# Softmax attention: key differences as units of the score ring, eight visits of 512 queries, head outputs added by GpSimd

## The reference

```
h = layernorm(x, ln1_g, ln1_b)
q, k, v = (h @ Wq), (h @ Wk), (h @ Wv)            # 16 heads of 16
scores = einsum('bqhd,bkhd->bhqk', q, k) / sqrt(16)
attn   = softmax(scores, axis=-1)                  # over 4096 keys
ctx    = einsum('bhqk,bkhd->bqhd', attn, v)
x = x + ctx @ Wo
```

## Time and profile before

| | us |
|---|---|
| median of 3 runs (lowest, highest) | 3835.98 (3832.73, 3839.26) |
| the profiled execution's own time | 3843.38 |
| its span | 3841.6 |
| PE busy | 3525.6 (92%) |
| DVE busy | 2883.9 (75%) |
| ACT busy | 2607.8 (68%) |
| POOL busy | 735.7 (19%) |
| mean granted TensorE clock | 0.944 |

### The profile page before, as it was taken

One profiled execution on the slowest core, in us unless ns is written; L12 is line 12 of the kernel. 1 busy time (PEld: TensorE's weight loads), 2 busy tenths in 40 slices (PEclk: granted clock), 3 DMA queues, 4 the chain that ended last, 5 costly groups with the idle time before them and its releaser, 6 DMA issues. The chain is left out here.

```text
span 3841.6 us, 86736 instructions
## 1 busy us (share of the span) xinstructions
PE 3525.6 (92%) x29108; PEld 1910.1 (50%) x29108; DVE 2883.9 (75%) x5446; ACT 2607.8 (68%) x3034; POOL 735.7 (19%) x735
## 2 busy tenths in 40 slices
PE   7979999999999999999999999999998807999990
PEld 4534444444444444444444444444443706999980
DVE  1767999999999999999999999999994522333335
ACT  2427888888888888888888888888887104555540
POOL 0300000000000000000000000000000367888856
PEclk8958999999999999999999999999999758999995
DMA  3630101010110101011010101101001524444424
GB/s 108 219 66 11 26 12 26 14 24 14 24 26 13 25 14 24 14 24 26 14 24 14 24 14 26 24 14 24 13 13 49 180 102 140 139 139 137 137 86 131
DMA packets 159912, 206.72 MB, mean 54 GB/s; under 512 B 50177, under 2 KB 123777, under 8 KB 154369
## 3 DMA queue, kind: packets, MB, share of 16 engines
q1 hardware_dynamic: 141136, 173.78, 16.7%
q0 software_dynamic: 6336, 16.79, 1.4%
q10 hardware_dynamic: 12144, 12.06, 0.9%
HBM read 134.59 MB, written 66.85 MB: 52 GB/s over the span
## 5 line engine op out<-in xcount | busy, mean ns | idle before, releaser
L759 ACT ACTIVATE probs<-s_ps 128x1024 f32<-128x1024 f32 x2048 | 2056.4, 1026 | 419.4 <-PE s_ps L678 391.8
L793 DVE TENSOR_REDUCE unit_max<-m_ps 128x1 f32<-128x512 f32 x3584 | 2249.8, 685 | 66.4 <-PE m_ps L670 66.2
L693 PE MATMUL o_ps<-probs,v_here 128*32 128x256 f32 (+1 forms) x15360 | 1290.3, 408 | 0.6 <-ACT probs L759 0.6
L678 PE MATMUL s_ps<-q_stage,k_ring 50*128 50x512 f32 x4096 | 1028.7, 495 | 0.5
L670 PE MATMUL m_ps<-k_ring,q_stage 48*128 48x512 f32 x3840 | 966.3, 423 | 42.3 <-DMA q_stage<-qs_dram 21.5
L678 PEld LDWEIGHTS s_ps<-q_stage,k_ring 50*128 50x128 f32 x4096 | 385.9, 185 | 771.4 <-issue 650.1
L670 PEld LDWEIGHTS m_ps<-k_ring,q_stage 48*128 48x128 f32 x3840 | 621.2, 188 | 159.1 <-DVE unit_max L793 134.2
L693 PEld LDWEIGHTS o_ps<-probs,v_here 128*32 128x32 f32 x15360 | 303.8, 108 | 510.1 <-issue 507.1
L614 POOL TENSOR_TENSOR neg_max<-no_max,tile_max 128x4 f32<-128x4 f32 x127 | 25.5, 201 | 2461.8 <-DVE tile_max L808 2461.8
L1526 DVE TENSOR_TENSOR hidden_low<-h_ps,hidden_high 128x512 fp32r<-128x512 f32 x184 | 127.3, 692 | 366.5 <-ACT hidden_high L1490 366.5
L1486 ACT ACTIVATE h_ps<-h_ps,b_here 128x512 f32<-128x512 f32 x184 | 121.4, 660 | 255.3 <-PE h_ps L1423 255.3
(11 more groups left out here) (181 smaller groups left out, 2412.8 us busy)
## 6 DMA issues: line engine op xcount, KB each, us to landing
w_in<-in_W SPq DMA_DIRECT2D x46, 1024.0 KB, 4.9
q_stage<-max_turned SPq DMA_DIRECT2D x2048, 0.5 KB
q_stage<-qs_dram SPq DMA_DIRECT2D x768, 32.0 KB, 1.8
k_ring<-ks_dram SPq DMA_DIRECT2D x96, 128.0 KB, 4.3
slots_dram<-zero_rows SPq DMA_DIRECT2D x24, 512.0 KB, 6.7
rows_e<-slots_dram SPq DMA_DIRECT2D x24, 512.0 KB, 3.9
y_slots_dram<-y_out ACTq DMA_DIRECT2D x23, 512.0 KB, 4.2
qs_dram<-parts SPq DMA_DIRECT2D x16, 512.0 KB, 2.9
```

Of the source, the lines that this page charges most:

```text
L678: last = nc.tensor.matmul(s_ps[:, t % 2, k, :], k_ring[at:at + AROWS, par, P * t:P * t + P], q_stage[at:at + AROWS, buf * CHUNK:buf * CHUN ...
L693: last = nc.tensor.matmul(o_ps[at:at + SQ, lo:hi], v_here[:, par, first_tile(t) + 2 * k, :], probs[:, t, k, lo:hi], start=(pair == 0), sto ...
L759: nc.scalar.activation(probs[:, t, :, :], s_ps[:, t % 2, :, :], ACT.Exp).then_inc(exp_done, 1)
L793: nc.vector.tensor_reduce(unit_max[:, b, qt, 2 * j + k:2 * j + k + 1], m_ps[:, block_of(t, k) % 3, :], AX.X, ALU.max).then_inc(m_read, 1 + ...
```

## The change

**The differences.** Only query tiles 0 and 1, with the first group of 512 columns of differences of each side pairing, use them now: `differences` computes two score-like units a chunk (four matmuls of 512 columns: for query tile u, on the first side rows, differences of 512 keys, on the other side rows, differences of the next 512). They go through `s_ps`, not `m_ps`: the ring of scores has 18 units a chunk (`RING_UNITS`), and ScalarE takes relu of 1024 columns at once. Four blocks (`partners`) are what the relus are added to. The maxima ring has 28 blocks a chunk (`BLOCKS`) in place of 33, 24 of them plain. So key differences are needed for the first half of the keys only (`DIFF_CHUNKS` is 4).

**The visits.** Eight a chunk, all of 512 queries, one for each pair of units.

**The column groups.** `turn_o`, its bank and VectorE's copy are gone. After ScalarE's copy into `o_here`, SyncE moves row groups 1 to 3 to partition 0 on (`align`, three DMAs), GpSimd adds them in three instructions (`sum_o`), and SyncE stores with two DMAs.

**The maxima rows.** `max_turned` goes to DRAM in one DMA, and after its arrival four DMAs bring the rows into `q_stage`.

**The order.** TensorE's order of a chunk is a written list. ScalarE's copy comes after unit 2, not unit 8; tile maximum and transposition on VectorE come after plain pairs 3 and 5.

```diff
+KD_COLS = CHUNK
+DIFF_CHUNKS = 2 * KD_COLS // HALF
+DIFFS = 2
-VISITS = ((0, 0, CHUNK),) + tuple((p, lo, lo + HALF) for p in range(1, UNITS // 2) for lo in (0, HALF))
-SLOTS = tuple(range(10, 25))
-RELU_PAIRS = (1, 3)
-RING_BLOCKS = 2 * UNITS + 1
+VISITS = UNITS // 2
+PLAIN = (2, 3, 6, 7, 8, 9, 10, 11, 12, 13, 14, 15)
+BLOCKS = 2 * (UNITS - DIFFS)
+PARTNER_AT = (20, 22)
+RING_UNITS = UNITS + DIFFS
+DIFF_AT = (0, 4)
...
+            def differences(n, u):
+                par, at_ring = n // CHUNKS % 2, diff_place(n, u)
+                col = n % Q_BUFS * CHUNK + P * u
+                if at_ring > 1:
+                    pe.wait_ge(s_read, at_ring - 1)
+                for k, at in enumerate((0, TOP_ROW)):
+                    last = nc.tensor.matmul(s_ps[:, at_ring % 2, k, :], q_stage[at:at + SROWS, col:col + P],
+                                            kd_ring[at:at + SROWS, par, :], start=True, stop=True)
+                last.then_inc(s_done, 1)
...
+            def partners(n, u):
+                max_block(n, PARTNER_AT[u], 0, KCH * u + 1)
+                max_block(n, PARTNER_AT[u] + 1, 1, KCH * u)
...
+            def chunk(i):
+                n = i + LEAD
+                load_waits(n)
+                differences(n, 0)
+                pe.wait_ge(rows_in, (i + 1) * ROW_DMAS)
+                scores(i, 0)
+                plain(n, 0)
...
+            def sum_o(n):
+                pool.wait_ge(o_aligned, n * (16 * (P // SQ - 1)) + 16 * (P // SQ - 1))
+                pool.wait_ge(ctx_out, n * (2 * 16) + 2 * 16)
+                nc.gpsimd.tensor_tensor(ctx_stage[:, :], o_here[0:O_COLS, :], o_groups[:, 0, :], ALU.add).then_inc(o_added, 1)
+                pool.wait_ge(o_added, n * 2 + 1)
+                nc.gpsimd.tensor_tensor(ctx_stage[:, :], ctx_stage[:, :], o_groups[:, 1, :], ALU.add).then_inc(o_added, 1)
+                pool.wait_ge(o_added, n * 2 + 2)
+                nc.gpsimd.tensor_tensor(ctx_stage[:, :], ctx_stage[:, :], o_groups[:, 2, :], ALU.add).then_inc(o_summed, 1)
...
             def copy_o(i):
-                act.wait_ge(pv_done, i * len(VISITS))
+                act.wait_ge(pv_done, i * VISITS)
+                act.wait_ge(o_summed, i)
...
             def rows(n, buf):
                 sp.wait_ge(max_ready, n + 1)
+                sp.dma_start(dram["maxima"], max_turned[:, :, :]).then_inc(maxima_out, 16)
+                sp.wait_ge(maxima_out, n * 16 + 16)
                 for at in (0, TOP_ROW):
                     for r in range(MROWS):
                         row = q_stage[at + SROWS + r:at + SROWS + r + 1, ds(buf * CHUNK, CHUNK)].bitcast(F32)
-                        row = row.rearrange("a (t b n) -> a t b n", t=TPC, b=P // SQ)
-                        for b in range(P // SQ):
-                            sp.dma_start(row[:, :, b, :], max_turned[SQ * b:SQ * b + TPC, r, :]).then_inc(rows_in, 16)
+                        sp.dma_start(row.rearrange("a (t b n) -> a t b n", t=TPC, b=P // SQ),
+                                     dram["maxima"][:, r:r + 1, :].rearrange("(b s) r n -> r s b n", s=SQ)[:, 0:TPC, :, :]).then_inc(rows_in, 16)
```

More of the change, by code:

```diff
@@ L689, in values @@
-                pair, lo, hi = VISITS[visit]
+                if pair == 0 and i % CHUNKS == 0:
+                    pe.wait_ge(v_ready, i // CHUNKS + 1)
                 for t in (2 * pair, 2 * pair + 1):
@@ L692, in values @@
                         at = SQ * (2 * (t % 2) + k)
[L693 to L694 removed]
+                        last = nc.tensor.matmul(o_ps[at:at + SQ, :], v_here[:, par, first_tile(t) + 2 * k, :],
+                                                probs[:, t, k, :], start=(pair == 0), stop=(pair == VISITS - 1),
@@ new lines, in chunk_without_maxima @@
+            def chunk_without_maxima(i):
+                pe.wait_ge(rows_in, (i + 1) * ROW_DMAS)
+                for t in range(3):
+                    scores(i, t)
+                values(i - 1, 7)
+                for pair in range(VISITS - 1):
+                    for t in (2 * pair + 3, 2 * pair + 4):
+                        if t < UNITS:
+                            scores(i, t)
+                    values(i, pair)
+            for n in range(LEAD):
+                maxima_alone(n)
+            for i in range(RING - LEAD):
+                chunk(i)
@@ L739, in _ @@
+            for i in range(RING - LEAD, RING):
+                chunk_without_maxima(i)
+            values(RING - 1, 7)
         @block.scalar
@@ L741, in _, with differences @@
             act.preload_act_table(ACT.Exp)
-            def excess_pair(n, t):
-                act.wait_ge(m_done, n * (2 * UNITS) + (2 * t + 1))
-                nc.scalar.activation(excess[:, :], m_ps[:, block_of(t, 0) % 3, :], ACT.Relu).then_inc(excess_ready, 1)
+            def differences(n, u, place):
+                act.wait_ge(s_done, place + 1)
+                if not (isinstance(n, int) and n == 0):
+                    act.wait_ge(m_read, n * BLOCKS + (PARTNER_AT[u] + 2 - BLOCKS))
+                nc.scalar.activation(excess[:, u, :, :], s_ps[:, (DIFF_AT[u] if not isinstance(place, int) else place) % 2, :, :],
+                                     ACT.Relu).then_inc(s_read, 1)
@@ L763, in _ @@
             for n in range(LEAD):
-                for t in RELU_PAIRS:
-                    excess_pair(n, t)
-            chunk(0, True, first=True)
+                for u in range(DIFFS):
+                    differences(n, u, diff_place(n, u))
+            chunk(0, first=True)
             with act.Fori(1, RING - LEAD) as i:
-                chunk(i, True)
+                chunk(i)
             for i in range(RING - LEAD, RING):
-                chunk(i, False)
+                for t in range(3):
+                    exponential(i, t, score_place(i, t), score_place(i, t) % 2)
+                copy_o(i)
+                for t in range(3, UNITS):
+                    exponential(i, t, score_place(i, t), score_place(i, t) % 2)
@@ L843, in _, with plain @@
-            chunk(RING + 2, 0, ahead=False, finish=False, stores=RING // 2 - 1)
+            def plain(n, phase, b, r):
+                qt, j = PLAIN[r] // KCH, PLAIN[r] % KCH
+                for k in range(2):
+                    at = plain_at(r) + k
+                    dve.wait_ge(m_done, n * BLOCKS + (at + 1))
+                    nc.vector.tensor_reduce(unit_max[:, b, qt, 2 * j + k:2 * j + k + 1], m_ps[:, (phase + at) % 3, :],
+                                            AX.X, ALU.max).then_inc(m_read, 1)
@@ new lines, in partners @@
+            def partners(n, phase, b, u, place):
+                dve.wait_ge(s_read, place + 1)
+                for k in range(2):
+                    at, j = PARTNER_AT[u] + k, 1 - k
+                    dve.wait_ge(m_done, n * BLOCKS + (at + 1))
+                    dve.sem_inc(dve_passed, 1)
+                    nc.vector.tensor_tensor_reduce(excess[:, u, j, :], m_ps[:, (phase + at) % 3, :], excess[:, u, j, :], 1.0, LEAST,
+                                                   ALU.add, ALU.max, unit_max[:, b, u, 2 * j:2 * j + 1]).then_inc(m_read, 1)
@@ new lines, in chunk @@
+            def chunk(n, phase, b, places, finish=True):
+                for r in range(3):
+                    plain(n, phase, b, r)
+                if finish:
+                    tile_maxima(n - 1, 1 - b)
+                for r in range(3, 5):
+                    plain(n, phase, b, r)
+                if finish:
+                    turn_maxima(n - 1)
+                for r in range(5, 10):
+                    plain(n, phase, b, r)
+                for u in range(DIFFS):
+                    partners(n, phase, b, u, places[u])
+                plain(n, phase, b, 10)
+                plain(n, phase, b, 11)
```

416 lines of the change are left out of this document (206 added, 210 removed).

## The result

| | before | after |
|---|---|---|
| median of 4 runs, us | 3835.23 | 3939.59 |
| lowest, highest | 3832.73, 3839.26 | 3932.32, 3941.16 |
| ratio (95% interval) | | 1.0264 (1.0245 to 1.0282) |
| span of the profiled execution | 3841.6 | 3939.4 |
| mean granted clock | 0.944 | 0.926 |

The change made the kernel 2.6% slower, 104 us. The forecast was 3763 with a range to 3840; it was wrong.

A forecast was written before the change was run, and what follows sets the result against it. PE was taken to set the pace: 18.0 us of steps plus 2.45 of waits, taken as 20.4 a chunk against 20.92, saves 64 us; with 9 outside, 73 off the 3835.98 median gives 3763, 80% range 3690 to 3840.

The forecast's parts named there:

- The other engines: ScalarE's and VectorE's work in a chunk: 17.0 us and 17.3 us, with VectorE's wait for ScalarE's relu gone.
- The granted clock falls below 1.00 in the steady state: Sign named beforehand: if the clock fell so in the attention's steady stage, the forecast is wrong.
- The rest of PE's chunk: TensorE's 32 steps a chunk other than visits, priced one by one; with the visits 18.0 us without waits, against 19.93.
- rival 3: No gain: a visit of 512 costs 1.14 us, chunk 20.9, time 3827; chance 0.11.
- New waits: Waits of TensorE that the new order brings: 2.45 us a chunk in three places, bringing the chunk to 20.45, taken as 20.4.
- (a): Chunk start: scores 1 wait 0.75 us for the relu, scores 2 another 0.4 for exponential 0.
- (b): Pairs with no visit between: the second one's banks are still being read, 0.25 us each, 1.0 in all.
- rival 2: Slower: maxima banks cost 0.72 us at each of five second pairs, 3.6 a chunk; 21.4 a chunk gives 3886; chance 0.13.
- (c): Near the chunk's end, scores 15 wait behind scores 13 and 14: 0.3 us.
- Hidden work: GpSimd's additions, alignment and maxima-row DMAs stay covered: 9 to 12 us and 17.1 us against 20.4; nothing charged for contention.
- Outside the steady state: Maxima alone -3, half-clock stage -3, fewer key differences -3, attention's end 0 to +3: sum -9 us.
- the 64.1 us at half clock: Stage at half clock holding 1.4 chunks with visits; the change was to save 3 us there.

The follow-up runs named there:

- new order: Changed kernel with first scores, plain pair and differences ahead of the leftover visit, pairs set apart: 3808.86 us with VectorE's three-chunk body, 3836.06 with six (the 20 stops).

## Why the prediction was wrong

**The step that failed: VectorE's loop was put at nothing.** "The other engines" counts VectorE's instructions in a chunk, 17.3 us, and takes it for granted that they follow one another; the loop around them isn't in the sum. The body went from two chunks to six, which the kernel's text shows (two buffers of `unit_max` times three banks). 2.1 us of stop in each of 21 rounds, and the clock's fall behind it, are 90 us; the forecast's gain of 73 would not have outlived them. "The granted clock falls below 1.00 in the steady state" stood among the signs that would prove it wrong, and came.

Without the stops the prediction would have been wrong too: 3849, outside its range. There a chunk is 17.1 of steps, 3.8 of waits and 0.2 of lower clock, 21.1 in place of 20.4.

**"The rest of PE's chunk": too high.** Forecast 18.0 without waits, measured 17.1. A score unit to the next step is 0.24 where no visit stood ahead of it, not 0.31 (12 of them, -0.8), a unit ahead of a visit 0.33, not 0.40 (-0.3); six pairs behind a visit are 0.34, not 0.29 (+0.3), the rest is rounding. The 0.43 came from the last chunks, which by the prediction's own words ScalarE sets. Visits came out as forecast, 1.00, and rival 3 (1.14) falls.

**"New waits": too low.** (a) the start of the chunk, 1.15 forecast, 1.4 measured, and its mechanism right: the relu and then exponential 0 gate scores 1 and 2. (b) second blocks, 1.0 forecast, 1.4 measured at the same four places (rival 2 counts five). It assumed that VectorE's lower load shortens these waits; in the kernel before with eight visits three banks and the blocks between two visits set them, at a VectorE busy for 82%. (c) 0.3 forecast at scores 15, 1.0 measured, since scores 7 and 11 wait as well. 3.8 in place of 2.45 took back what the steps gave, and the undisturbed chunk is 20.93, not 20.4. That is rival 2's mechanism, at 1.4 us a chunk in place of its 3.6.

**The clock stood among the signs and not in the sum.** Even without stops, the waits at a chunk's start were followed by 3 us at half clock every five chunks or so, 0.2 a chunk, 25 us. Cutting the relus short removed all of it, moving the first beside a visit half.

**"Hidden work": right.** No wait of PE for the maxima rows, none of ScalarE for GpSimd; an addition took 1.27 us, at the lower end, and contention wasn't seen. The store of the maxima landed after 2.7 us, as the 2.8 of the earlier trace rows had it, and not after the 2.0 that the prediction gives beside it. The alignment's DMAs took 5 us, not 2.8, which only attention's end shows.

**"Outside the steady state": -9 forecast, -13 measured, by terms that missed both ways.** I divide at the second copy and at the fourth from the end. The second comes 33.2 us earlier (303.27 against 336.49); 8 of these (6 of 16 units of a 20.9 us chunk) are only the copy's earlier place in a chunk, so the start gave 25. Six of them lie ahead of the first exponential (256.50 against 262.71), as forecast. The other 19 are the clock's, where "the 64.1 us at half clock" had -3. After:

```profile
261.50:325.60 64.10, 62.45 (x384) 22.54 (x376) 52.32 (x100) 52.40 (x57) 8.73 (x12) 0.97 0.18 32
```

It was 0.50 there in the earlier trace rows. The clock rose at 266 in place of 326. Ahead of it, in 223.2 to 261.5, PE was busy for 38.04 us, and for 35.91 in the kernel before; more is not shown. The traced execution of the kernel before was a late one: in three other kernels with its start (the bodies of four and six chunks, the eight visits) the clock rose at 282 to 290. At the end, from the fourth copy from the last to the projection's first DMA, it is 12 more (64.3 against 52.0), and 8 of these are again the copy's place: +4, forecast 0 to +3. And the stages behind attention took 7.7 longer in this execution (885 to 887 us in three of the fifteen traces, 875 to 883 in the others), which stays open. The steady state between lost 111 us.

Open, too: why the clock stayed low for 7 to 55 us behind most stops in the kernel before with the long body and for 3 to 10 us elsewhere, so what a stop costs (1.3, 4.3 or 9.5 us a round) was measured but could not have been computed.

## What to carry to other kernels

Where a change makes the body of an engine's loop longer, count its instructions and look in the new trace for one idle time per round that nothing explains; a third buffer that halves the body was worth 2.3% here. Ask of larger pieces on TensorE what then stands between them: four blocks for three banks cost more than any piece's price. And put a result that the next steps wait for ahead of the longest step that doesn't need it: the order written so, with the pairs set apart as well, turned the same work from 0.3% slower into 0.5% faster than the kernel before. Where the loop cannot be shortened, a long step of TensorE ahead of the work that VectorE would hold up hides most of a stop: 1.3 us a round in place of 4.3.

## What the runs showed of the hardware

- A branch back in VectorE's loop of 393 or 421 instructions stopped it for 1.8 to 2.1 us; 143, 198 and 282 instructions and straight code did not.
- TensorE's clock fell to 0.5 behind 20 of 20 stops of VectorE for which PE stood still 1.8 us on average (changed kernel), and behind 7 of 20 for which it stood still 0.2 to 0.4 us (new order). It also fell every 100 us or so behind a chunk's start with 1.4 us of short waits, but never in the kernel whose PE idled 0.3 us of every 2.94 throughout.
- On TensorE, two sets of four-group matmuls of 256 columns back to back cost 1.00 us, as one of 512 does; with other steps between, each costs 0.57.
- A wait whose value comes from a register makes ScalarE start 0.07 us later than one on a constant (0.62 against 0.55).
